# A pipelined state-space layer with an MLP: skip products first, one transpose group moved, one product given to VectorE

## The reference, cut to what matters

```python
cumlog = jnp.cumsum(lz, axis=1)
A = exp(cumlog[:, :, None] - cumlog[:, None, :])            # causal
S_intra = einsum('btshk,bshp->bthpk', A * bc[:, :, None], xc)
S_total = exp(cumlog) * state + S_intra
y = einsum('bthk,bthpk->bthp', cc, S_total).real
y = y + x_ssm * D
g = y * silu(z)
g = g * rsqrt(mean(g * g) + eps) * norm_w
x = x + g @ out_proj_w.T + mlp(xn)
```

## Time and profile before

| | us |
|---|---|
| median of 3 runs (lowest to highest) | 327.7 (325.67 to 329.19) |
| the profiled execution | 327.39 |
| its span | 325.6 |
| busy in the span: PE, DVE, ACT, POOL | 291.6, 256.1, 190.4, 191.0 |
| share of PE in the chain that ended last | 65% |

### The profile page before, as it was taken

The page is one execution under the profiler, slowest core; times in us unless marked ns, Lnnn a source line. Parts: engine busy times, 40 slices in busy tenths (PEclk is TensorE's granted clock), DMA queues, the critical chain, the costliest instruction groups (busy, mean ns, idle before and its releaser), DMA issues.

```text
span 325.6 us, 9422 instructions
## 1 busy us (share of the span) xinstructions
PE 291.6 (90%) x3903; PEld 211.9 (65%) x3903; DVE 256.1 (79%) x627; ACT 190.4 (58%) x350; POOL 191.0 (59%) x165
## 2 busy tenths in 40 slices
PE   2299865979999999999999999999999999988984
PEld 2145423567768776777767876787687768764774
DVE  4481388979888988898889988989889887798941
ACT  0662397519764777557854886488548765574110
POOL 1000316432999279944997399929991999179201
PEclk9755599799999999999999999999999999999996
DMA  7400140012201330123011311132012301230101
GB/s 186 123 1 0 27 105 0 0 36 67 67 0 35 81 84 2 35 59 86 24 32 42 85 41 34 34 84 49 2 35 60 74 0 35 52 81 2 35 2 41
DMA packets 19464, 14.99 MB, mean 46 GB/s; under 512 B 5108, under 2 KB 15192, under 8 KB 19416
## 3 DMA queue, kind: packets, MB, share of 16 engines
q1 hardware_dynamic: 17208, 13.83, 16.4%
q10 hardware_dynamic: 2208, 0.49, 0.8%
HBM read 3.83 MB, written 2.10 MB: 18 GB/s over the span
## 4 chain that ended last, share of the span: by engine, by line
PE 65%; DVE 13%; POOL 7%; ACT 5%; issue 5%; DMA 2%; SPq 1%; DVEq 0%; ACTq 0%; POOLq 0%
PE bank L1546 11%; PE bank L1598 7%; PE bank L1599 7%; PE bank L1609 4%; PE bank L1649 4%; PE bank L1656 3%; PE bank L1619 3%; PE bank L1729 3%; PE bank L1700 3%; PE bank L1685 3%; PE bank L1629 2%; ACT z L1140 2%; PE bank L1572 2%; POOL btmp L1390 2%; PE bank L1587 1%
## 5 line engine op out<-in xcount | busy, mean ns | idle before, releaser
L1386 POOL TENSOR_TENSOR btmp<-cims,X 128x512 f32<-128x512 f32 x15 | 19.1, 1272 | 57.9 <-ACT X L1157 57.3
L1598 PE MATMUL bank<-h0h,W 128*128 128x512 f16 x128 | 49.5, 387 | 3.8 <-DVE h1l L836 2.0
L1546 PE MATMUL bank<-XW,xh 128*128 128x256 f16 x256 | 49.8, 291 | 0.0
L1599 PE MATMUL bank<-h0l,W 128*128 128x512 f16 x128 | 49.5, 387 | 0.0
L1546 PE MATMUL bank<-XW,xl 128*128 128x256 f16 x128 | 37.3, 291 | 0.0
L1190 ACT ACTIVATE h1h<-bank 128x512 f16<-128x512 f32 x32 | 18.9, 593 | 25.1 <-PE bank L1599 25.1
L1360 POOL TENSOR_TENSOR xd<-x,dt 128x1024 f32<-128x1024 f32 x8 | 15.2, 1902 | 28.7 <-ACT x L1101 28.1
L1546 PEld LDWEIGHTS bank<-XW,xh 128*128 128x128 f16 x256 | 26.6, 104 | 7.5 <-issue 2.6
L1146 ACT ACTIVATE tin<-bank,base 128x256 f32<-128x256 f32 x16 | 6.7, 471 | 35.6 <-PE bank L1572 35.5
L1598 PEld LDWEIGHTS bank<-h0h,W 128*128 128x128 f16 x128 | 13.7, 107 | 19.1 <-DVE h1l L836 3.0
L836 DVE SCALAR_TENSOR_TENSOR h1l<-bank,h1h 128x512 f16<-128x512 f32 x32 | 21.8, 685 | 5.1 <-ACT h1h L1190 5.0
(11 more groups left out here) (200 smaller groups left out, 851.3 us busy)
## 6 DMA issues: line engine op xcount, KB each, us to landing
xtok<-in_x SPq DMA_DIRECT2D x8, 256.0 KB, 3.4
cims<-bc SPq DMA_DIRECT2D x32, 64.0 KB, 2.1
cres<-bc SPq DMA_DIRECT2D x32, 64.0 KB, 2.4
bres<-bc SPq DMA_DIRECT2D x32, 64.0 KB, 2.1
bims<-bc SPq DMA_DIRECT2D x32, 64.0 KB, 2.1
out<-osb SPq DMA_DIRECT2D x7, 256.0 KB, 2.3
const<-constants SPq DMA_DIRECT2D x1, 512.0 KB, 7.4
KT<-in_in_proj_w ACTq DMA_DIRECT2D x1, 320.0 KB, 4.2
```

The lines of the kernel that those rows point to most:

```text
L1386: P.tensor_tensor(btmp[1][:], b[:], f2, ALU.mult).then_inc(sig.sem, 1)
L1546: last = M.matmul(dst, tok(x, c, k), w[:, k, :], start=False, stop=True, skip_group_check=True)
L1598: M.matmul(banks[f][:], w, h0h[:, k, :], start=(k == 0), stop=False)
L1599: last = M.matmul(banks[f][:], w, h0l[:, k, :], start=False, stop=(k == MT - 1))
```

## The change

On TensorE, in turns 1 to 7, K's third chunk is transposed right behind the first two, into bank 1 and no longer into bank 5, ahead of the wait for z. Then all four `skipped` products open y's banks, `new_states` follows (behind waits for the copies of K, for x dt and for the third mask), and behind the remaining masks come all four `within` products and `from_state`. In turns 1 to 6, the product of Kre and B's imaginary row moves from GpSimd to VectorE (`k_re_times_b`, behind `final`, ahead of `h1_low(n, 2)`, into `tmpb`), with a new semaphore `s_kb` on which GpSimd waits before it subtracts.

```diff
@@ VectorE @@
+            def k_re_times_b(n):
+                v.wait_ge(b_in.sem, b_in.done(n))
+                v.wait_ge(s_bk.sem, s_bk.at(n, 0))
+                V.tensor_tensor(subs(tmpb), subs(Kre), view(bims, 0, 128, SUB - 1, [[SUB, NSUB], [0, SUB]]),
+                                ALU.mult).then_inc(s_kb, 1)
...
                 final(n - 1, pq, stored)
+                k_re_times_b(n)
                 h1_low(n, 2)
                 h1_low(n, 3)
                 decayed(n, 2)
@@ ScalarE, kt_copies @@
-                    step(a_kt, A.copy(KT[:, 2, :, :], bank[5][:, 0:256]))
+                    step(a_kt, A.copy(KT[:, 2, :, :], bank[1][:, 0:256]))
@@ GpSimd @@
+            def b_and_k_rest(n):
...
+                P.tensor_tensor(subs(btmp[0]), subs(Kim), view(bres, 0, 128, SUB - 1, [[SUB, NSUB], [0, SUB]]),
+                                ALU.mult).then_inc(s_bk.sem, 1)
+                g.wait_ge(s_bk.sem, s_bk.at(n, 4))
+                g.wait_ge(s_kb, n)
+                P.tensor_tensor(Bim[:], btmp[0][:], tmpb[:], ALU.subtract).then_inc(s_bk.sem, 2)
+                g.wait_ge(s_bk.sem, s_bk.at(n, 6))
...
                     b_and_k(n, s_kq, 0)
-                    b_and_k(n, s_kq, 1)
+                    b_and_k_rest(n)
@@ TensorE @@
                     k_transposes((0, 1), bank[0])
-                    y_wait(b, True, n if has_front else b)
-                    k_transposes((2,), bank[5])
-                    within(1 - p, 0)
-                    skipped(1 - p, 0)
-                    within(1 - p, 1)
-                    skipped(1 - p, 1)
+                    k_transposes((2,), bank[1])
+                    pe.wait_ge(a_silu.sem, a_silu.done(n))
+                    for c in range(NCH):
+                        skipped(1 - p, c, True)
                     pe.wait_ge(a_kt.sem, a_kt.done(b))
+                    pe.wait_ge(s_xd.sem, s_xd.done(b))
+                    pe.wait_ge(s_g[True].sem, s_g[True].at(b, 3))
                     new_states(1 - p)
-                    for c in (2, 3):
-                        within(1 - p, c)
-                        skipped(1 - p, c)
+                    y_wait(b, True, n)
+                    for c in range(NCH):
+                        within(1 - p, c, False)
```

More of the change, by code:

```diff
@@ L335, in build @@
         s_im = signal("imaginary_halves", 6)
+        s_kb = sem("K_real_times_B")
         s_rot = signal("C_rotated", 6)
@@ L1428, in b_and_k, with subs @@
                 g.wait_ge(s_bk.sem, s_bk.at(n, 6 if half else 3 * part + 3))
+            def b_and_k_rest(n):
+                def subs(t):
+                    return t[:].rearrange("p (c t) -> p c t", t=SUB)
+                P.tensor_tensor(subs(btmp[0]), subs(Kim), view(bres, 0, 128, SUB - 1, [[SUB, NSUB], [0, SUB]]),
[4 more added lines that the diff above has]
+                g.wait_ge(s_bk.sem, s_bk.at(n, 6))
             def pipelined(n, has_back, has_front, has_next):
```

## The result

| | before | after |
|---|---|---|
| median of 20 runs, us | 326.97 | 324.47 |
| lowest to highest, us | 325.03 to 332.86 | 319.65 to 329.13 |
| profiled execution, us | 327.39 | 323.43 |
| its span, us | 325.6 | 321.6 |
| first `g_across` of turn 1, us | 71.64 | 69.58 |

The change made the kernel faster, by 2.5 us (0.8%) between the medians of all runs. The ratio of the comparison is 0.9875 (95% interval 0.9838 to 0.9912), 4.1 us; it counts only runs within 1.5% of each kernel's fastest (16 of before, 10 of after), and after has the wider spread downwards, which is why it says more than the medians. The forecast was 1.3 us less, at 326.1, range 324.6 to 329.8; the measured median lies 0.13 us under the range.

A forecast was written before the change was run, and what follows sets the result against it. The prediction took TensorE's own order, without idle time, as the bound. Gains of 2.3 us (2.1 + 0.13 + 0.09) less 1.0 for VectorE's product gave -1.3 against the profiled 327.39: 326.1 us, range 324.6 to 329.8.

The forecast's parts named there:

- TensorE's stop before y: Third chunk's transposes needlessly behind the wait for z; moving them saves 0.35 us per turn, 2.1 us over turns 1 to 6.
- the order itself: y's products on TensorE, same in number and shape, skip products first: costed at nothing.
- Turn 7 gains nothing: In turn 7 VectorE does the gate long after y ended, so the gain there was taken as 0.
- GpSimd's late Bim: Product off GpSimd brings Bim about 0.5 us earlier: gains 0.13 us in turn 3, 0.09 in turn 4 through x dt.
- VectorE's product: Added product waits for GpSimd's instruction and delays `lora1`: 0.79 us in turn 3, 0.20 in turn 4, 1.0 in all.
- the release + 1.08: When `h1_low(n, 3)` can start after GpSimd's instruction releases the shared port; wanted at 27.53 us behind `g_across`.
- two signs that were named: `g_across` starts about 34.6 us apart in turn 3; rows of `k_re_times_b` longer than 0.68 in turns 2 to 4.
- rivals 4: No contest: VectorE's product gets through in every turn; 325.1 us, chance 0.12.
- Rival 5: More saved than rows show: turn 7 gains too, a stop hides in modelled matmul ends; about 324 us, chance 0.04.
- Rival 1: VectorE misses the gap in turns 1, 5, 6, waits one GpSimd product, 0.75 us each; 328.3 us, chance 0.22.
- Rival 2: GpSimd keeps the port over two products; U and `lora1` come 1.76 us late; 331.4 us, chance 0.10.
- Rival 3: y's gain is given back at `from_state`, waiting for VectorE's states, margin 0.17 us; 328.2 us, chance 0.10.

The follow-up runs named there:

- transposes_only: Kernel before, only K's third chunk transposed into bank 1 ahead of the wait for z, y's products in the old order; median 324.44 us.
- order_only: Kernel before with all skip products first, then states, then within products; third chunk's transposes left behind the wait in bank 5; median 327.24 us.
- as_before: Kernel before, unchanged, run once more as a control; median 326.76 us.
- pe_only: Kernel after with K's product back on GpSimd, so TensorE's new order alone; median 324.13 us.
- as_after: Kernel after, unchanged, run once more; median 324.92 us.
- dve_only: Kernel before with only K's product moved from GpSimd to VectorE; median 328.85 us.
- behind_low2: Kernel after with the VectorE product one place later, behind `h1_low(n, 2)`; median 326.36 us.
- doubled: Kernel after with the VectorE product made twice in a row, the first into a tile nobody reads; median 333.31 us.
- behind_u: Kernel after with the VectorE product behind U (`decayed(n, 2)`), ahead of the taps; median 324.68 us.
- u_first_pe: Kernel after with K's product back on GpSimd and U (`decayed(n, 2)`) moved ahead of `h1_low(n, 3)`; median 324.17 us.

## Why the prediction was right or wrong

- **TensorE's stop before y.** Right in kind and size: 0.35 us per turn forecast, 0.36 to 0.38 measured in the four turns that nothing else touches, and `transposes_only` and `order_only` show which of the edits carries it. That the order itself costs and gains nothing held as well.
- **Turn 7 gains nothing.** Right: the gate follows 12.14 us behind `g_across` (284.86 in VectorE's timeline of after, less 272.72), before 12.14 too (289.09 less 276.95).
- **GpSimd's late Bim.** Its 0.13 us in turn 3 and 0.09 in turn 4 were to come back. Turn 4 did (34.27 to 33.82), but it is 33.82 in `transposes_only` and 34.19 in `order_only` as well, without the relief, so that the 0.09 are not shown to be its work; nor are the 0.13, since turn 3 of `as_before` took 34.18 as it is. What the relief does is not in the sum: it keeps x dt off the layer norm (0.36 us in turn 3 of `transposes_only`, 0.27 in `pe_only`), and it shortens the delay when a copy of C lands late (1.72 in turn 4 of `pe_only`).
- **The mis-sized term: VectorE's product, 1.0 us forecast, 0.25 measured.** The rule of the port held: with the sum of turn 3 ending at 163.91, 26.70 behind `g_across`, the release + 1.08 gives 27.78 where 27.53 is wanted, a delay of 0.25, and turn 3 is 0.25 longer than its neighbours. What failed is the input: I carried GpSimd's ends of turns 3 (27.24) and 4 (26.65) over from the trace of before, as if the change left them where they were; in after they are 26.70 and 26.07. They are not an accident of that execution, for they recur in `as_before` (27.03 and 26.66). That of turn 3 depends on a copy of C that was 1.15, 0.96 and 1.24 us late in before, `as_before` and `order_only`, and 0 to 0.64 in the other eleven traces. In those three the SP queue took 3.15 to 3.21 us to issue the four copies of C's imaginary part ahead of it, asked for 3.32 behind `g_across`; in the other eleven it took 2.38, asked for at the same time, and nine of them had a long issue (2.81 to 3.51 us) in turn 4 instead. So the delay moved with the schedule; why the issue is long in one turn and not in another stays open. That of turn 4 comes from the masks that GpSimd's x dt had held up, behind the late turn 3. Together this is 0.75 us. It is also why two signs that were named failed: turn 3 took 34.07 and not about 34.6, and the product's row in turn 4 has its bare 0.68.
- **The base.** I subtracted from the profiled execution's 327.39; the median of 20 runs of before is 326.97, 0.4 us lower. The two together: 326.97 less the 2.17 us that the traces show in turns 1 to 6 is 324.8; the median of after is 324.47. The remaining 0.3 us stays open; in another series the medians of the same two kernels were 327.23 (before) and 324.92 (after), 2.3 us apart, against 2.5 here. But the difference by the ratio, 4.1 us (2.9 to 5.3 by its interval), does not contain the 2.17, and no run shows where more would come from: the stretch ahead of turn 1 differs between executions of one and the same kernel.
- **The range.** It began at 324.6 because the sum of all gains without any cost gave 325.1. It held the mechanism's time (327.39 less 2.17 is 325.2) but left too little for the scatter of the base. With the product's cost at the measured 0.25 the sum would have given 325.3. The measured time lies between the numbers of rivals 4 (325.1) and 5 (about 324), and neither mechanism happened: their numbers are near by luck.
- **The rivals.** Rival 1 (a missed gap costs one GpSimd product) is real: it is turn 1 of `as_after` and four turns of `dve_only`. Rival 2 (two products) is excluded by `behind_low2`, `dve_only` and `doubled`: the Trainium skill's rule that the lock is held for one instruction ("SBUF — State Buffer", "SBUF: two separate sides") is what these traces show. Rival 3 did not happen in after; it happened in one turn each of `transposes_only`, `pe_only`, `behind_u` and `u_first_pe` (waits of 0.29, 0.21, 0.46 and 0.26 us at `from_state`), each time behind late masks. Rival 4 is wrong: the port is contested. Rival 5: no sign in turn 7, and the 2.06 us ahead of turn 1 aren't the change's, since `as_after` began turn 1 at 73.11, later than before.
- **What stays open.** Why VectorE's request at 26.08 wins the gap in after (the sum ends at 26.07 or 26.08, GpSimd's next product is recorded from 26.15 or 26.16) is plausible by the order of arrival, but no run moved the request in steps across the gap. The nearest rows are those of `dve_only`: in turn 2 VectorE got in, its product and GpSimd's both recorded from 26.46, in turn 1 it did not, 0.22 behind GpSimd's start (26.46 and 26.24).

## What to carry to other kernels

On an engine without idle time, look for work that stands behind a wait it does not need; its length behind the wait, and nothing else of the edit, is the gain. An instruction moved to another engine is priced by the queue behind it up to the next thing somebody waits for, and by what it shares with its neighbour; here the same product costs 0.4 us, 0 or 1.5 us in a turn by where it asks for the port. A delay read in the trace of before must be asked what sets it, before it is carried into a sum for the changed kernel: here it recurred in a second execution of before, and was elsewhere once the turns had another length.

## What the runs showed of the hardware

- **Sharing between VectorE and GpSimd** goes by whole instructions and alternates while both ask: a 0.68 us product took 1.54 or 1.55 us behind one GpSimd product of 1.06 in each turn of `doubled`, and GpSimd's two products of 1.06 took 1.39 to 1.54. A VectorE row of 128x4 with one input is held up too: 1.70 us for 0.17 beside GpSimd's x dt, in `transposes_only`.
- **The stretch ahead of turn 1 differs by 8.8 us between executions.** Turn 1 began at 64.65 (`transposes_only`) to 73.42 us (`behind_low2`) in the fourteen traces, at 71.64 and 69.70 in two executions of the kernel before, at 69.58 and 73.11 in two of after. Part of it is TensorE's clock. From 16 to 40 us it was granted 0.50 (the lower level, 1.2 GHz) in before and 1.00 (2.4 GHz) in after, where the change has not yet touched anything. But this record alone misleads: `dve_only` was granted 1.00 there too and began turn 1 at 71.56, as late as before. The windows of before, after and `dve_only`:

```profile
16.00:40.00 24.00, 21.98 (x91) 11.65 (x92) 11.15 (x38) 10.24 (x20) 3.25 (x3) 0.50 0.03 6
```

```profile
16.00:40.00 24.00, 20.70 (x99) 10.87 (x99) 12.46 (x42) 13.05 (x24) 4.08 (x3) 1.00 0.06 15
```

```profile
16.00:40.00 24.00, 21.99 (x91) 11.67 (x92) 11.16 (x38) 10.22 (x20) 3.25 (x3) 1.00 0.02 6
```

What tells them apart is the matmuls of z themselves, in the same order: a row of 512 columns takes 0.63 us in before and in `dve_only`, with the next one 0.42 to 0.43 behind it, and 0.38 in after, with the next 0.22 behind. After has rows of 0.63 as well, at 17 us and under a recorded 1.00, but fewer of them. The rows are those of before, after and `dve_only`:

```profile
38.34 0.63 PE L1564 MATMUL bank<-xl,ZW 128*128 128x512 f16 x1
```

```profile
35.49 0.38 PE L1584 MATMUL bank<-xl,ZW 128*128 128x512 f16 x1
```

```profile
38.33 0.63 PE L1584 MATMUL bank<-xl,ZW 128*128 128x512 f16 x1
```

A change of 0.36 us in each of six turns is plain in the trace and nearly lost in the time.
